# Two causal attention passes: a diagonal of four key tiles walked in three steps instead of four, in a loop unrolled over six groups

## The chip, the cores and the metric

One core of one Trainium2 chip runs the whole program. The metric is device microseconds (us) of one execution, lower is better.

## What is computed

Four residual stages on x of shape (8, 1024, 256): latent attention with softmax, a squared-ReLU MLP, an attention with a quadratic feature map, a ternary linear layer. The two attentions share one function of the kernel:

```python
scores = jnp.einsum('bqhd,bkhd->bhqk', Q, K) / math.sqrt(D_K)     # 16 heads of 16, 1024 positions
scores = jnp.where(causal, scores, -jnp.inf)
attn = jax.nn.softmax(scores, axis=-1)                            # first attention
out = jnp.einsum('bhqk,bkhd->bqhd', attn, V)
# second attention: features are the products x_i x_j, so phi_q . phi_k is a squared score,
# summed causally: num = sum_k (q.k)^2 v_k, den = sum_k (q.k)^2
```

## The kernel before

`attend_pass` works in 32 units (n), one for every batch and group of four heads. A unit holds 1024 queries in two halves h of 512 columns and eight key tiles kt of 128. Transposed scores (128 keys by up to 512 queries, one PSUM bank a head) are made for one **step**, which is one pair (h, kt). There are twelve: for h = 0 the tiles 0 to 3, all on the diagonal, 512, 384, 256 and 128 live columns wide (`q0(s)` is the first live one); for h = 1 the tiles 0 to 3 full, then 4 to 7 of 512, 384, 256 and 128. Engines hand over by semaphores, each engine's order is written out by hand:

- TensorE (PE), in iteration s of `unit`: `scores(s + 2, 0)` for heads 0 and 1, `scores(s + 2, 1)` for heads 2 and 3 (L996, bf16), then `weigh(s)`, the product of the weights with V (L1010, float32, four heads side by side in column groups). AHEAD = 2 steps lie between.
- ScalarE (ACT): `weights(s)` (L893), Exp in the first attention and Square in the second, two instructions a step; `take_sums` (L885) copies the output bank of a half to `osb` when the half's last `weigh` is done. In the order of ACT it stands behind `weights(n + 1, 1)`.
- GpSimd (POOL): one `affine_select` (L866) for each step that holds a diagonal block, eight a unit, on 128 columns of four heads; `weigh` waits for it.
- VectorE (DVE), second attention: the fourth head's square, as a copy (L925) and a product (L928). Steps use three pairs of score banks in turn.
- DVE, first attention: row maxima for the softmax of a later unit. PE makes 36 chunks of 512 columns a unit (`maximum_scores`, L985) into a ring of SRING = 3 banks, DVE reduces them (L946, L948), then `largest` (L954 to L962) finishes a unit's maxima.
- The chunks of later units are dealt into the PE program, one after each `scores` and each `weigh`, three a step. In unit n the first 18 belong to unit n + 1, the last 18 (EARLY = 9 pairs) to unit n + 2. Chunk 18 waits for the load of unit n + 2.
- SyncE (SP), in unit n: wait for the last `weigh` of unit n - 1, 15 transfers of unit n + 2 (L808; q and k parts, then `vs`), store of half 0 (L819), in the first attention 8 small transfers `load_rows` (L815) that carry the maxima to the operands of unit n + 1 once `largest` is done, store of half 1. PE waits for these rows before `scores(n + 1, 0)`.

`all_units` (L790) is a hardware loop of 10 trips with three units written out in each, since the operand tiles rotate by three, and two more units behind it.

Of the kernel before, what the change touches and what calls it, by code (L numbers as in the profile page):

```python
# [703 lines left out]
def attend_pass(nc, z, m, first, softmax):  # L704
# [7 lines left out]
    ROUNDS = (UNITS - 2) // RING  # L712
    assert UNITS == RING * ROUNDS + 2
    ROWS = STACK + 2 if softmax else STACK
# [6 lines left out]
    SLOTS = 4  # L721

# [8 lines left out]
    assert CH == 3 * STEPS  # L731
    SRING = 3
    EARLY = 9
    with ExitStack() as ctx:
# [45 lines left out]
        def q0(s):  # L780

            h, kt = steps[s]
            return max(0, kt * P - h * 512)

        def score_bank(s, hd):
            return 2 * ((2 * s + hd // 2) % PAIRS) + hd % 2

        def all_units(eng, unit):

            with eng.Fori(0, ROUNDS) as i:  # L790
                for r in range(RING):
                    unit(RING * i + r, r, i, True, True)
            unit(UNITS - 2, 0, ROUNDS, True, False)
            unit(UNITS - 1, 1, ROUNDS, False, False)

        @block.sync
        def _(sp):
# [23 lines left out]
            def unit(n, r, rnd, ahead, far):  # L821
# [23 lines left out]
        def _(pool):  # L845
# [14 lines left out]
            def unit(n, r, rnd, ahead, far):  # L860
                for d, s in enumerate(DIAG):
                    if not softmax:
                        pool.wait_ge(d_ready, STEPS * n + s + 1 + DR)
                    wait_alone(pool, p_ready, 2 * STEPS * n + 2 * s + 2 + PR, m.alone)
                    diag = p[s % SLOTS][:, :, q0(s):q0(s) + P]
                    pool.affine_select(out=diag, in_=diag, compare_op=ALU.is_ge, fill=0.0, base=0,  # L866
                                       pattern=[[0, HPU], [1, P]], channel_multiplier=-1).then_inc(masked, 1)
# [4 lines left out]
        def _(act):  # L872
# [9 lines left out]
            def take_sums(n, h):  # L882
                act.wait_ge(pv_done, STEPS * n + (4, STEPS)[h] + PV)
# [3 lines left out]
            def weights(n, s):  # L887
                act.wait_ge(pv_done, STEPS * n + s + 1)
                for k in range(2):
                    act.wait_ge(st_ready, 2 * STEPS * n + 2 * s + k + 1)  # L890
                    heads = 2 if softmax or k == 0 else 1
                    at = score_bank(s, 2 * k)
                    act.activation(p[s % SLOTS][:, 2 * k:2 * k + heads, q0(s):512], m.psum[:, at:at + heads, q0(s):512],  # L893
                                   ACT.Exp if softmax else ACT.Square, scale=z.DK ** -0.5).then_inc(p_ready, 1)

            def unit(n, r, rnd, ahead, far):
                for s in range(STEPS):
                    if s + AHEAD < STEPS:
                        weights(n, s + AHEAD)
                    elif ahead:  # L900
                        weights(n + 1, s + AHEAD - STEPS)
                    if s == 3:
# [3 lines left out]
            for s in range(AHEAD):  # L906
                weights(0, s)
# [3 lines left out]
        def _(dve):  # L911
# [5 lines left out]
            if not softmax:  # L917
                dve.sem_inc(d_ready, DR)

                def unit(n, r, rnd, ahead, far):  # L920

                    for s in range(STEPS):
                        dve.wait_ge(st_ready, 2 * STEPS * n + 2 * s + 2)
                        bank = m.bank[score_bank(s, 3)][:, q0(s):512]
                        dve.tensor_copy(twin[s % 2][:, q0(s):512], bank).then_inc(twin_ready, 1)  # L925
                        dve.wait_ge(pv_done, STEPS * n + s + 1)
                        dve.wait_ge(twin_ready, STEPS * n + s + 1)
                        dve.scalar_tensor_tensor(out=p[s % SLOTS][:, 3, q0(s):512], in0=bank, scalar=1.0 / z.DK,  # L928
                                                 in1=twin[s % 2][:, q0(s):512], op0=ALU.mult, op1=ALU.mult
# [35 lines left out]
            def unit(n, r, rnd, ahead, far):  # L965
# [12 lines left out]
        def _(pe):  # L978
# [10 lines left out]
            def scores(n, r, s, k):  # L989
                h, kt = steps[s]  # L990
# [3 lines left out]
                for hd in (2 * k, 2 * k + 1):  # L994
                    live = operand_rows(hd)
                    last = pe.matmul(m.bank[score_bank(s, hd)][:, q0(s):512], ks[r][live, hd, kt * P:(kt + 1) * P],  # L996
                                     qs[r][live, hd, h * 512 + q0(s):(h + 1) * 512], start=True, stop=True)
                last.then_inc(st_ready, 1)

            def weigh(n, r, s):  # L1000
# [833 lines left out]
```

## Time and profile before

| | us |
|---|---|
| median of 3 runs (2956.73 to 2960.54) | 2957.39 |
| the profiled execution's own time | 2961.86 |
| its span, first to last instruction | 2959.7 |
| mean granted clock of TensorE | 0.938 |
| first attention (a_ tiles), loop and tail | about 300 to 1216 |
| second attention (b_ tiles), loop and tail | about 2087 to 2692 |

The engines are PE (matmul), PEld (weight load, overlaps PE), DVE, ACT, POOL and SP. Matmuls are pipelined and their ends are modelled, so the starts of two neighbouring groups, not their lengths, say what a group takes. In the timeline, "idle before" with a releaser is the engine's own idle time and what ended it; "issue" means that nothing the profile shows was waited for.

### The profile page before, as it was taken

The numbers are of one execution on the slowest core, as the hardware profiler recorded it, in microseconds if no ns is written. First come the engines' busy times: TensorE is split into PE (matmuls) and PEld (weight loads), VectorE is DVE, ScalarE is ACT, GpSimd is POOL, SyncE is SP. The second block draws the span as 40 slices with busy tenths as digits, with TensorE's granted clock in tenths as the row PEclk, the third lists the DMA queues.
The fourth block names the chain that finished last, engine by engine and source line by source line (L and its number), as shares of the span: only waits on it lengthen the run. The fifth ranks groups of instructions, "written<-read, shape, count | busy, mean of one in ns | idle before, by whom it ended". The sixth has DMA issues, their size and how long they took to land. (4 is left out here: it accounts for less than half of the span.)

```text
span 2959.7 us, 60061 instructions
## 1 busy us (share of the span) xinstructions
PE 2508.8 (85%) x15239; PEld 1160.4 (39%) x15239; DVE 2276.6 (77%) x5893; ACT 1784.9 (60%) x2938; POOL 577.6 (20%) x650
## 2 busy tenths in 40 slices
PE   2687999999999999577999978884899999995656
PEld 1342333333333333254666655553222222222545
DVE  5887888888888888286777767997667666665968
ACT  0452666666666666315777747664677777773446
POOL 0445111111121111230000001222222222222300
PEclk9897999999999999888999999997899999997879
DMA  5495232332323322240000003445644444442403
GB/s 169 155 286 187 83 92 89 91 93 86 107 80 100 94 86 79 85 168 1 0 0 0 0 1 100 156 146 167 161 142 141 137 136 139 140 127 99 142 15 113
DMA packets 243316, 309.97 MB, mean 105 GB/s; under 512 B 39472, under 2 KB 177408, under 8 KB 243200
## 3 DMA queue, kind: packets, MB, share of 16 engines
q1 hardware_dynamic: 242752, 307.50, 33.6%
q10 hardware_dynamic: 448, 1.31, 0.2%
q14 instruction: 91, 0.75, 0.1%
q8 instruction: 25, 0.41, 0.1%
HBM read 181.29 MB, written 126.88 MB: 104 GB/s over the span
## 5 line engine op out<-in xcount | busy, mean ns | idle before, releaser
L893 ACT ACTIVATE a_p<-psum 128x1024 f32<-128x1024 f32 (+3 forms) x768 | 588.1, 813 | 303.0 <-PE psum L996 298.4
L893 ACT ACTIVATE b_p<-psum 128x512 f32<-128x512 f32 (+5 forms) x768 | 453.5, 654 | 164.4 <-PE psum L996 163.5
L948 DVE CUSTOM_DVE_ANT_0 a_dump<-psum,a_bias 128x128 bf16<-128x128 f32 (+3 forms) x1024 | 445.6, 487 | 105.7 <-PE psum L985 74.4
L996 PE MATMUL psum<-b_qs,b_ks 96*128 96x512 bf16 (+7 forms) x1536 | 320.9, 330 | 36.0 <-DMA b_vs<-values 35.7
L946 DVE TENSOR_REDUCE a_peak<-psum 128x1 f32<-128x512 f32 x512 | 326.1, 685 | 21.7 <-PE psum L985 20.2
L1010 PE MATMUL psum<-b_p,b_vs 128*32 128x512 f32 (+3 forms) x3072 | 328.5, 499 | 8.0 <-POOL b_p L866 8.0
L925 DVE COPY b_twin<-psum 128x512 f32<-128x512 f32 (+3 forms) x384 | 213.5, 556 | 146.6 <-PE psum L996 144.9
L985 PE MATMUL psum<-a_ks,a_qs 112*128 112x128 bf16 (+2 forms) x1008 | 294.0, 336 | 37.9 <-DVE a_peak L948 19.9
L866 POOL TENSOR_SCALAR_AFFINE_SELECT a_p<-a_p 128x512 f32<-128x512 f32 x256 | 162.4, 635 | 767.2 <-ACT a_p L893 767.2
L866 POOL TENSOR_SCALAR_AFFINE_SELECT b_p<-b_p 128x512 f32<-128x512 f32 x256 | 162.4, 634 | 455.2 <-DVE b_p L928 440.2
L996 PE MATMUL psum<-a_qs,a_ks 114*128 114x512 bf16 x1008 | 248.0, 328 | 3.4 <-ACT a_p L893 1.8
L928 DVE SCALAR_TENSOR_TENSOR b_p<-psum,b_twin 128x512 f32<-128x512 f32 (+3 forms) x384 | 214.5, 558 | 40.0
L996 PEld LDWEIGHTS psum<-b_qs,b_ks 96*128 96x128 bf16 (+1 forms) x1536 | 110.1, 98 | 339.9 <-issue 173.7
L1444 PE MATMUL psum<-f_xt,w_fc 128*128 128x512 f32 x512 | 223.9, 595 | 4.7 <-ACT f_hid L1385 2.8
L1010 PE MATMUL psum<-a_p,a_vs 128*32 128x512 f32 x2016 | 218.8, 507 | 0.6 <-POOL a_p L866 0.4
L1246 PE MATMUL psum<-wo,m_att 128*128 128x256 f32 x512 | 142.3, 441 | 77.0 <-POOL m_att L1193 74.1
L1580 POOL TENSOR_TENSOR g_parts<-g_rest,g_parts 128x2048 bf16<-128x2048 f32 x16 | 65.2, 4074 | 667.1 <-DVE g_parts L1568 667.1
L985 PEld LDWEIGHTS psum<-a_ks,a_qs 112*128 112x128 bf16 x1008 | 87.2, 97 | 260.3 <-DVE a_peak L948 124.4
L985 PE MATMUL psum<-first_k,first_q 112*128 112x128 bf16 (+3 forms) x528 | 159.3, 348 | 30.1 <-DMA first_v<-values 16.6
L1455 PE MATMUL psum<-w_proj,f_parts 128*128 128x256 bf16 x1536 | 170.3, 273 | 1.4 <-DVE f_scaled L1333 1.4
L1455 PEld LDWEIGHTS psum<-w_proj,f_parts 128*128 128x128 bf16 x1536 | 150.2, 98 | 19.4 <-DVE f_scaled L1333 1.7
L1246 PEld LDWEIGHTS psum<-wo,m_att 128*128 128x128 f32 x512 | 112.8, 226 | 102.8 <-issue 52.4
(202 smaller groups left out, 3752.8 us busy)
## 6 DMA issues: line engine op xcount, KB each, us to landing
qk_parts<-l_parts SPq DMA_DIRECT2D x96, 256.0 KB
qk_parts<-g_parts SPq DMA_DIRECT2D x96, 256.0 KB, 2.8
b_qs<-qk_parts SPq DMA_DIRECT2D x160, 128.0 KB, 2.9
b_ks<-qk_parts SPq DMA_DIRECT2D x155, 128.0 KB, 2.9
values<-l_vx SPq DMA_DIRECT2D x64, 256.0 KB
sums<-a_osb SPq DMA_DIRECT2D x64, 256.0 KB, 2.4
m_num<-sums SPq DMA_DIRECT2D x64, 256.0 KB
m_inv<-reciprocals SPq DMA_DIRECT2D x64, 256.0 KB
```

Source lines behind the costliest of these rows:

```text
L866: pool.affine_select(out=diag, in_=diag, compare_op=ALU.is_ge, fill=0.0, base=0, pattern=[[0, HPU], [1, P]], channel_multiplier=-1).then_i ...
L893: act.activation(p[s % SLOTS][:, 2 * k:2 * k + heads, q0(s):512], m.psum[:, at:at + heads, q0(s):512], ACT.Exp if softmax else ACT.Square, ...
L925: dve.tensor_copy(twin[s % 2][:, q0(s):512], bank).then_inc(twin_ready, 1)
L928: dve.scalar_tensor_tensor(out=p[s % SLOTS][:, 3, q0(s):512], in0=bank, scalar=1.0 / z.DK, in1=twin[s % 2][:, q0(s):512], op0=ALU.mult, op ...
L946: last = dve.tensor_reduce(dst, piece, AX.X, ALU.max)
L948: last = dve.tensor_tensor_reduce(dump[c % SRING][:, at:at + w], piece, bias[:, 512 - w:], 1.0, NEG, ALU.add, ALU.max, dst)
L985: last = pe.matmul(m.bank[SB + c % SRING][:, at:at + w], qs[r][0:TOP, hd, qt * P:(qt + 1) * P], ks[r][0:TOP, hd, h * 512:h * 512 + w], sta ...
L996: last = pe.matmul(m.bank[score_bank(s, hd)][:, q0(s):512], ks[r][live, hd, kt * P:(kt + 1) * P], qs[r][live, hd, h * 512 + q0(s):(h + 1) ...
L1010: last = pe.matmul(m.bank[OB[h]][32 * hd:32 * hd + 32, q0(s):512], vs[r][:, kt, 32 * hd:32 * hd + 32], p[s % SLOTS][:, hd, q0(s):512], sta ...
L1246: last = pe.matmul(bank, att[u][:, c, t * P:(t + 1) * P], wo[:, c, :], start=(c == 0), stop=(c == DC - 1))
L1444: last = pe.matmul(m.bank[F0 + j % 4], m.w_fc[:, c, j * P:(j + 1) * P], xt[u][:, c, :], start=(c == 0), stop=(c == DC - 1))
L1455: last = pe.matmul(bank, parts[u][:, part, j, t * P:(t + 1) * P], m.w_proj[:, j, :], start=(part == j == 0), stop=(part == PARTS - 1 and j ...
```

## The change

Steps 1 and 3 of a diagonal (384 and 128 columns) become one step of 512: its bank holds tile kt + 1 in columns 128 to 512 and tile kt + 3 in columns 0 to 128. The order of a diagonal is full, merged, 256. Ten steps a unit instead of twelve. One ACT pair, one DVE pair and one `pv_done` serve both pieces; PE still issues a matmul for each piece and head, POOL still masks each diagonal block on its own, so a merged step has two masks, the second behind a wait for the first. Chunks of the maxima are dealt (1, 2, 1) to eight steps and (1, 1, 0) to the two narrow ones; the first 20 of a unit belong to unit n + 1, the last 16 (EARLY = 8) to unit n + 2. Four weight tiles and three bank pairs no longer repeat within one unit or three, so the loop has 5 trips of six units.

```diff
-    ROUNDS = (UNITS - 2) // RING
-    steps = [(h, kt) for h in range(2) for kt in range(4 * (h + 1))]
+    LONG = 2 * RING
+    ROUNDS = (UNITS - 2) // LONG
+    def full(h, kt):
+        return h, ((kt, 0, 0, 512),)
+    def edge(h):
+        kt = 4 * h
+        return [full(h, kt), (h, ((kt + 1, 128, 128, 384), (kt + 3, 0, 384, 128))), (h, ((kt + 2, 256, 256, 256),))]
+    steps = edge(0) + [full(1, kt) for kt in range(4)] + edge(1)
     STEPS = len(steps)
-    DIAG = [s for s, (h, kt) in enumerate(steps) if kt >= 4 * h]
+    LAST = (2, STEPS - 1)
+    DIAG = [[at for kt, at, q, w in pieces if kt >= 4 * h] for h, pieces in steps]
+    MASKS = [sum(len(d) for d in DIAG[:s + 1]) for s in range(STEPS)]
...
-    EARLY = 9
+    EARLY = 8
+    MOST = [(1, 1, 0) if s in LAST else (1, 2, 1) for s in range(STEPS)]
...
             with eng.Fori(0, ROUNDS) as i:
-                for r in range(RING):
-                    unit(RING * i + r, r, i, True, True)
+                for v in range(LONG):
+                    unit(LONG * i + v, v, 2 * i + v // RING, True, True)
...
-                for d, s in enumerate(DIAG):
+                for s in range(STEPS):
+                    if not DIAG[s]:
+                        continue
                     if not softmax:
                         pool.wait_ge(d_ready, STEPS * n + s + 1 + DR)
                     wait_alone(pool, p_ready, 2 * STEPS * n + 2 * s + 2 + PR, m.alone)
+                    for k, at in enumerate(DIAG[s]):
+                        if k:
+                            wait_alone(pool, masked, MASKS[-1] * n + MASKS[s] - 1, m.alone)
+                        diag = slot(v, s)[:, :, at:at + P]
+                        pool.affine_select(out=diag, in_=diag, compare_op=ALU.is_ge, fill=0.0, base=0,
+                                           pattern=[[0, HPU], [1, P]], channel_multiplier=-1).then_inc(masked, 1)
...
                 for hd in (2 * k, 2 * k + 1):
                     live = operand_rows(hd)
+                    for kt, at, q, w in pieces:
+                        last = pe.matmul(m.bank[score_bank(v, s, hd)][:, at:at + w], ks[r][live, hd, kt * P:(kt + 1) * P],
+                                         qs[r][live, hd, h * 512 + q:h * 512 + q + w], start=True, stop=True)
...
-                if s in DIAG:
-                    pe.wait_ge(masked, len(DIAG) * n + DIAG.index(s) + 1)
+                if DIAG[s]:
+                    pe.wait_ge(masked, MASKS[-1] * n + MASKS[s])
...
+                for kt, at, q, w in pieces:
+                    for hd in range(HPU):
+                        last = pe.matmul(m.bank[OB[h]][32 * hd:32 * hd + 32, q:q + w], vs[r][:, kt, 32 * hd:32 * hd + 32],
+                                         slot(v, s)[:, hd, at:at + w], start=(kt == 0), stop=(s == LAST[h]),
+                                         skip_group_check=True)
...
+                    late = CH - 2 * EARLY
+                        if k < late and ahead:
+                            maximum_scores(n + 1, (r + 1) % RING, 2 * EARLY + k, 2 * EARLY + k + 1)
+                        if k >= late and far:
+                            if k == late:
+                                pe.wait_ge(loaded[(r + 2) % RING], LOADED * (rnd + (r + 2) // RING) + LOADED)
+                            maximum_scores(n + 2, (r + 2) % RING, k - late, k - late + 1)
...
+                    for k in range(3):
+                        if k == 2:
+                            weigh(n, v, s)
+                        elif there:
+                            scores(*at, k)
+                        some_maxima(dealt, MOST[s][k])
+                        dealt += MOST[s][k]
```

## Rows read from the trace of the kernel before

**Rows 1.** By stretch: length, PE, PEld, DVE, ACT, POOL busy (x), PEclk, DMA, GB/s
```profile
346.00:1185.50 839.50, 787.35 (x5574) 282.55 (x5578) 715.23 (x2437) 554.77 (x755) 147.22 (x232) 0.98 0.30 90
573.20:576.60 3.40, 3.40 (x15) 1.02 (x8) 2.33 (x13) 0.74 (x1) 0.52 (x1) 0.50 0.66 188
655.70:740.20 84.50, 79.78 (x577) 28.95 (x576) 73.64 (x253) 57.20 (x79) 15.07 (x25) 1.00 0.31 94
2297.97:2354.55 56.58, 55.86 (x432) 15.94 (x433) 39.35 (x73) 44.69 (x79) 15.22 (x24) 1.00 0.46 139
```

**Rows 2.** L954 from 340 to 1190 us: once a unit
```profile
L954 DVE TENSOR_REDUCE a_npeak<-a_peak x30: 220/220/221, 346.0 to 1185.5; 128x32 f32<-128x64 f32 x30
```

**Rows 3.** Waits from 400 to 1170 us: us in total, times, longest
```profile
DVE a_dump L948 <- issue: 21.9, 14, 2.8
PE psum L985 <- DMA first_v<-values: 14.9, 9, 2.0
```

**Rows 4.** Timeline of the first attention, from one unit's load to its use
```profile
623.59 0.64 PE L1010 MATMUL psum<-a_p,a_vs 128*32 128x256 f32 x8
626.31 0.60 ACT L885 ACTIVATE a_osb<-psum 128x512 f32<-128x512 f32 x1
627.80 0.63 SPq L808 DMA_DIRECT2D a_qs<-qk_parts  x1
637.47 0.44 SPq L808 DMA_DIRECT2D a_vs<-values  x1
641.68 4.99 SPq L815 DMA_DIRECT2D first_q<-a_rows  x8
642.19 0.39 PE L985 MATMUL psum<-a_ks,a_qs 112*128 112x128 bf16 x2 [2.04 <-DMA a_vs<-values]
650.54 0.39 PE L985 MATMUL psum<-a_ks,a_qs 112*128 112x512 bf16 x1
652.16 0.64 PE L1010 MATMUL psum<-a_p,a_vs 128*32 128x256 f32 x8
```

**Rows 5.** DMA issues from 400 to 1170 us: KB each, median us to landing
```profile
q14 instruction: 51, 0.42, 0.2%
a_qs<-a_rows SPq DMA_DIRECT2D x144, 2.0 KB, 1.8
```

**Rows 6.** Timeline behind two ends of a trip, first attention
```profile
572.00 0.39 PE L985 MATMUL psum<-a_ks,a_qs 112*128 112x512 bf16 x1 [1.98 <-DVE a_peak L948]
...
658.27 0.29 DVE L948 CUSTOM_DVE_ANT_0 a_dump<-psum,a_bias 128x128 bf16<-128x128 f32 x1 [2.50 <-issue]
```

**Rows 7.** Timeline of the second attention, one full step, then the end of a unit
```profile
2305.88 1.06 PE L1010 MATMUL psum<-b_p,b_vs 128*32 128x512 f32 x8
2306.88 1.04 PE L996 MATMUL psum<-b_qs,b_ks 96*128 96x512 bf16 x4
2307.85 1.06 PE L1010 MATMUL psum<-b_p,b_vs 128*32 128x512 f32 x8
2307.95 0.69 DVE L925 COPY b_twin<-psum 128x512 f32<-128x512 f32 x1 [0.48 <-PE psum L996]
2308.75 0.69 DVE L928 SCALAR_TENSOR_TENSOR b_p<-psum,b_twin 128x512 f32<-128x512 f32 x1
2309.68 0.63 POOL L866 TENSOR_SCALAR_AFFINE_SELECT b_p<-b_p 128x512 f32<-128x512 f32 x1 [8.72 <-DVE b_p L928]
2315.55 0.43 PE L1010 MATMUL psum<-b_p,b_vs 128*32 128x128 f32 x8
2316.83 1.07 PE L1010 MATMUL psum<-b_p,b_vs 128*32 128x512 f32 x8 [0.24 <-POOL b_p L866]
```

**Rows 8.** DMA queues from 2140 to 2650 us: the only line of part 3
```profile
q1 hardware_dynamic: 28192, 71.14, 45.8%
```

**Rows 9.** ACT from 400 to 1170 us by shape: busy, mean ns
```profile
L893 ACT ACTIVATE a_p<-psum 128x1024 f32<-128x1024 f32 x323 | 315.9, 1026 | 142.5 <-PE psum L996 142.3
L893 ACT ACTIVATE a_p<-psum 128x768 f32<-128x768 f32 x107 | 81.0, 808 | 29.1 <-PE psum L996 25.2
```

More of the change, by code:

```diff
@@ L819, in store, with unit @@
                 sp.dma_start(m.sums_dram[bass.ts(n, P), h * 512:(h + 1) * 512], osb[h][:, :]).then_inc(stored[h], 16)
-            def unit(n, r, rnd, ahead, far):
+            def unit(n, v, rnd, ahead, far):
+                r = v % RING
                 if far:
@@ L858, in _, with unit @@
                 pool.wait_ge(k_set, 2)
-            def unit(n, r, rnd, ahead, far):
-                for d, s in enumerate(DIAG):
+            def unit(n, v, rnd, ahead, far):
+                for s in range(STEPS):
+                    if not DIAG[s]:
+                        continue
                     if not softmax:
@@ L906, in _ @@
             for s in range(AHEAD):
-                weights(0, s)
+                weights(0, 0, s)
             all_units(act, unit)
@@ L963, in largest, with unit @@
                               ).then_inc(rows_ready, 1)
-            def unit(n, r, rnd, ahead, far):
+            def unit(n, v, rnd, ahead, far):
+                r = v % RING
                 if ahead:
@@ L987, in maximum_scores, with scores @@
                     last.then_inc(s_ready, 1)
-            def scores(n, r, s, k):
-                h, kt = steps[s]
+            def scores(n, v, s, k):
+                h, pieces = steps[s]
+                r = v % RING
                 pe.wait_ge(p_ready, 2 * STEPS * n + 2 * s + k + 1)
@@ L995, in scores, with weigh @@
                     live = operand_rows(hd)
[L996 to L997 removed]
+                    for kt, at, q, w in pieces:
+                        last = pe.matmul(m.bank[score_bank(v, s, hd)][:, at:at + w], ks[r][live, hd, kt * P:(kt + 1) * P],
+                                         qs[r][live, hd, h * 512 + q:h * 512 + q + w], start=True, stop=True)
                 last.then_inc(st_ready, 1)
[L1000 to L1001 removed]
+            def weigh(n, v, s):
+                h, pieces = steps[s]
+                r = v % RING
                 pe.wait_ge(p_ready, 2 * STEPS * n + 2 * s + 2 + PR)
@@ L1018, in operands, with unit, some_maxima @@
                     pe.wait_ge(rows_loaded[r], ROWS_LOADED * rnd + ROWS_LOADED)
-            def unit(n, r, rnd, ahead, far):
-                def some_maxima(k):
+            def unit(n, v, rnd, ahead, far):
+                r = v % RING
+                def some_maxima(first, count):
                     if not softmax:
                         return
-                    half = CH // 2
-                    if k < half and ahead:
-                        maximum_scores(n + 1, (r + 1) % RING, half + k, half + k + 1)
-                    if k >= half and far:
-                        if k == half:
-                            pe.wait_ge(loaded[(r + 2) % RING], LOADED * (rnd + (r + 2) // RING) + LOADED)
-                        maximum_scores(n + 2, (r + 2) % RING, k - half, k - half + 1)
+                    late = CH - 2 * EARLY
+                    for k in range(first, first + count):
+                        if k < late and ahead:
[4 more added lines that the diff above has]
+                            maximum_scores(n + 2, (r + 2) % RING, k - late, k - late + 1)
+                dealt = 0
                 for s in range(STEPS):
```

69 lines of the change are left out of this document (28 added, 41 removed).

## The prediction

> **What bounds the kernel now.** First I read the busy time of one trip in each attention [rows 1]. In the second attention PE works 55.86 of 56.58 us for three units, 18.86 a unit; ACT has 44.69 and DVE 39.35. Only PE sets the pace there. In the first, PE works 79.78 of 84.50 us and DVE 73.64: neither is full, and the waits must say what the rest is.
>
> A unit of the first attention is the distance between two L954: 29 in 839.5 us, 28.95 each [rows 2]. It has three kinds of loss. PE stands up to 2.0 us before a chunk until the `vs` transfer has landed [rows 3]; the row shown has 9 cases with 14.9 us, that of the other buffers as many, so this comes in two units of three. DVE stands up to 2.8 us for "issue", 21.9 us over the eight trip ends of that stretch [rows 3]; the timeline shows it is the jump back of the loop, 2.50 us that nothing in the program ended, and PE then waits for DVE, 1.98 us in another trip [rows 6]. The two don't add up: where a trip end has held PE, the load has landed meanwhile. Third, behind some of these stalls the granted clock falls: after the 1.98 us at 572.00 it is 0.50 (1.2 GHz, else 2.4) from 573.2 to 576.6 [rows 1, 6]. Over the 29 units it is 0.98 [rows 1]: 4% of the time at half rate, 34 us, which cost half of that, 17 us.
>
> The load's chain is in [rows 4]. Let T be the end of a unit's last `weigh` but one: it starts at 623.59, its 256 columns take 0.46, T = 624.05. ACT reaches `take_sums` at 626.31 (T + 2.26), SP starts the 15 transfers at 627.80, issues the last at 637.47, and PE goes on at 642.19, T + 18.1, after 2.04 us of idle. With the mean stall of 14.9 / 9 = 1.65 it is T + 17.7. From there to the next T (652.16 + 0.46 = 652.6) are 10.4 us without a stall: 28.1 for a unit inside a trip. A unit behind a trip end has the 2.4 us of the jump instead of the 1.65: about 28.9. Check: 19 x 28.1 + 10 x 28.9 + 17 = 840, as measured.
>
> **First attention.** I count PE work in blocks of 512 columns, 0.213 us at 2.4 GHz. A step costs 0.26 us above its columns: 8 blocks in 2307.85 - 2305.88 = 1.97 us [rows 7]. About 0.07 of it belong to the matmuls; 0.19 are the two changes between scores and float32 product, which a merged step pays once for both pieces.
>
> *Removed:* two steps' changes, 0.38 us of PE a unit. The columns stay (108 blocks with the maxima).
>
> *Where the first chunk of unit n + 2 stands.* Before, PE reached it 18.1 - 2.04 = 16.1 us after T. After, 68 blocks stand between T and chunk 20: 8 of iteration 9, then 10, 12, 8, 12, 12 and 6 of iteration 5; 14.5 us, with six steps' extra 16.1. PE arrives at the same time. The load arrives later: ahead of `take_sums` ACT now has `weights(n + 1, 1)` at 1024 elements instead of 768, 1026 against 808 ns twice [rows 9], and its scores end later: 0.5 us. T to chunk 20 becomes 18.2, the stall about 2.
>
> *From there to the next T* are left 6 blocks of iteration 5, then 12, 10 and 11: 39 blocks, 8.3 us, 1.0 extra, 9.3 instead of 10.4. A unit inside a trip takes 27.5 instead of 28.1: PE stands still for the load with more of the unit done.
>
> *Trip ends.* Ten become five; I take 29.6 us for such a unit. The jump costs DVE the same 2.5. SP's chain, if its doubled loop has to be fetched too, adds up to 2.5 to the load. And the rows begin to bind: SP starts them at 641.68, the last is issued at 646.1 and lands 1.8 us later [rows 4, 5], near 647.6, 5.4 us after PE went on; PE asks at 650.54 now, 8.35 us after it went on, and 6.7 after the change. With a load stall ahead 1.3 us remain; without one about 1 us is missing.
>
> Over 29 units: 24 x 27.5 + 5 x 29.6 = 808 against 823, -15. Two chunks fewer ahead of the loop and four exponentials fewer in the last unit: -2. The clock: stalls of 2 us in 25 units instead of 1.65 in 20 let it fall somewhat more often; its price was 17 us for ten trip ends and twenty load stalls, I add +3 (bounds 0 and +15). **First attention: -14.**
>
> **Second attention.** *PE:* 72 blocks are 15.36 us, twelve steps' extra make 18.48; the 0.38 up to 18.86 are the wait of `weigh(0)` for its mask, at 2316.83 and in each unit [rows 7]. After: 18.10, and that wait goes, since 12 blocks instead of 8 stand between the scores of step 0 and `weigh(0)`.
>
> *A new wait, the merged step's two masks.* From the end of its scores (2306.88 + 0.87) it is 0.20 to the copy, 0.80 to the product, 0.93 to POOL, 0.63 for a mask [rows 7], a gap in which POOL waits for itself, 0.63, and 0.14 to PE. The gap isn't in these rows: below it is 0, above the 0.24 from DVE's end to POOL's start (2308.75 + 0.69 to 2309.68); I take 0.24, since it is a semaphore wait as well: 3.6 us. Between the scores of the unit's first merged step and its `weigh` PE has 12 blocks, with the changes 3.15 us: a stall of 0.4 (0.2 with no gap). The second has 14 blocks: none. Unit: 18.5 instead of 18.86; 31 units, **-11**. ACT (15 us a unit) and DVE (13) stay below.
>
> *The loop's body.* Of this I am least sure. A trip now issues 577 + 576 matmuls and weight loads in the first attention and 432 + 433 in the second [rows 1], plus some 60 waits a unit by the code. DVE issues 253 in the first and with its waits, two for each of 108 chunks and more, near 480. PE, ACT and SP stand nowhere at their jumps; DVE in the first attention does at each. The stretch of the first holds 51 instruction fetches [rows 5], that of the second none [rows 8]. So a short body stays inside an engine and a long one is fetched at each trip. Doubled, PE's is 2,300 + 340 and 1,730 + 300, more than any that stays here; ACT, SP and the second attention's DVE come to 300 to 360, between the 200 that stay and the 480 that doesn't. For PE's jump the bounds are 0, if it stays, and DVE's 2.8 at most in these rows; I take 2.5, by the nearest row. In the first attention it lies beside DVE's. In the second nothing hides it: 5 x 2.5 = +12.5, and the clock, which fell behind about a third of the long stalls, adds 1.7 in some: +3. The other engines' fetches fall into the same 2.5 us. **Together +4.5.**
>
> The Trainium skill, "Runtime: NRT & Kernel Launch", section "Instruction fetch mechanics", says that TensorE keeps 2048 instructions and the others 512, filled in order, and that a jump to a target outside stalls the engine. By that the first attention's body on PE falls out and the second's, about 2,030, could just stay; this sum would end 15.5 us lower. The trace agrees that a short body isn't fetched again, but DVE's of about 480, under the page's 512, is.
>
> **Sum.** -14 + 4.5 = -9.5 us; other stages are untouched. The terms come from an execution with a span of 2959.7 and a time of 2961.9, 4.5 above the median of 2957.4. Set against the median: 2948.
>
> **Rivals.**
> 1. *PE's doubled body stays in the second attention.* For it: no body of PE has fallen out so far. Against: it would be the longest of all by far. -9.5 - 15.5: 2932. Chance 0.18, with the page above for it.
> 2. *Jumps cost more.* Behind the first fetched block comes a second stall, or the stalls of PE, DVE, SP and ACT follow one another: 5 us instead of 2.5 in ten trip ends, +13 to +25: 2961 to 2973, slower. It decides from about 4 us a jump. For it: a longer body has more fetches. Against: DVE's never exceeds 2.8 [rows 3]. Chance 0.15.
> 3. *The rows become the bound.* Between the last chunk of a unit's maxima and its first scores PE has 6.9 us; the chain is 1.0 for that chunk, 1.1 for `largest`, 5.9 to the last landing, 8.0. It decides when the load stall ahead of it falls under 1 us or DVE is late by as much: +1 us in 25 units, 2973. For it: four chunks a step are 2.6 us of DVE in 2.8 of PE. Against: the load stall falls just there. Chance 0.08.
> 4. *The masks stall both merged steps*, with a gap of 0.6: +0.7 a unit, 2970. Chance 0.06.
>
> The forecast has 0.53, its own range is 2940 to 2956. Eight in ten: from rival 1, 2930, to where rivals 2 to 4 begin, 2965. 0.2% is 5.9 us, about what a measurement of this kernel can tell from none. Faster (below 2951.5): rival 1 and two thirds of the forecast, and a tenth of the others, 0.57. Slower (above 2963.3): most of rivals 2 to 4 at their high ends, 0.18. The same: 0.25.
>
> **What the profile after would show.** In the second attention: full steps 1.97 us apart as before, no wait of `weigh(0)` for POOL, one of 0.4 us before `weigh(1)`, units of 18.5; at five trip ends a PE gap of about 2.5 us, with instruction fetches in the loop. In the first: units of 27.5 inside a trip with a `vs` wait of about 2 us, five DVE gaps of 2.5, L815 landing before PE asks. The prediction is wrong if a wait for rows stands before the scores of each unit, if PE has no gap at its jumps, or if the gaps are 5 us.

## The result

The changed kernel takes 2995.6 us (median of 4 runs, 2978.6 to 3000.1) against 2957.1 (4 runs): ratio 1.012 [1.0085, 1.0155]. It is slower by 38.5 us between the medians, where 2948 was forecast, and it lies outside the range, above the price of every rival too (2973 at most). The profiled execution is the fastest of the four: 2978.6 us, span 2976.9, only 17.2 more than the span before. The other runs lie 16 to 22 us above it; most of this spread gets an explanation below.

The copies of the output bank (`a_osb` and `b_osb`) frame each attention. Before, first and last start of the 64:

```profile
L885 ACT ACTIVATE a_osb<-psum x64: 597/603/628, 313.6 to 1216.0; 128x512 f32<-128x512 f32 x64
L885 ACT ACTIVATE b_osb<-psum x64: 597/603/605, 2096.1 to 2692.1; 128x512 f32<-128x512 f32 x64
```

After:

```profile
L905 ACT ACTIVATE a_osb<-psum x64: 597/605/606, 310.6 to 1238.7; 128x512 f32<-128x512 f32 x64
L905 ACT ACTIVATE b_osb<-psum x64: 597/605/608, 2116.1 to 2711.6; 128x512 f32<-128x512 f32 x64
```

The first attention took 902.4 us and takes 928.1; the second took 596.0 and takes 595.5. So +25.7 and -0.5, where -14 and +4.5 were forecast. What lies around them is 8 us shorter in this execution: 1453.3 us for 1461.3. A second profile of the same kernel (e4_again below) has 1463.0 there, so this is no effect of the change.

Windows with the same columns as in [rows 1], after (a stretch of the first attention; the 3.4 us behind a PE gap in the second and in the first; one unit of the second; one trip of six units of the first):

```profile
346.00:1185.50 839.50, 767.80 (x5422) 284.16 (x5426) 717.97 (x2380) 521.30 (x621) 144.40 (x228) 0.97 0.30 90
2222.20:2225.60 3.40, 3.40 (x15) 0.76 (x14) 1.09 (x3) 0.87 (x2) 1.91 (x3) 0.51 0.16 55
856.60:860.00 3.40, 3.40 (x18) 1.31 (x11) 1.81 (x9) 0.88 (x1) 0.00 (x0) 0.54 0.04 3
2183.30:2201.60 18.30, 18.14 (x149) 5.75 (x146) 12.74 (x21) 14.67 (x24) 4.99 (x8) 1.00 0.45 145
657.00:837.90 180.90, 165.17 (x1152) 60.83 (x1152) 152.70 (x504) 111.05 (x132) 31.01 (x49) 0.96 0.29 89
```

A trip of the first attention has 1152 + 1152 = 2,304 matmuls and weight loads on PE. One of the second, six units, has 1,728:

```profile
2220.30:2334.00 113.70, 109.98 (x864) 34.36 (x864) 76.78 (x122) 88.31 (x134) 30.03 (x49) 0.98 0.46 141
```

The granted clock fell to half in the second attention too, where before it stood at 1.00.

Waits from 400 to 1170 us, to be held against [rows 3]:

```profile
PE psum L1008 <- DMA a_vs<-values: 30.6, 17, 3.7
PE psum L1008 <- DMA first_v<-values: 16.1, 9, 2.2
```

And the second attention, 2140 to 2650 us. "issue" at the first scores of a trip is PE's jump; at one of the four jumps the profile names DVE instead, which came last:

```profile
PE psum L1021 <- issue: 7.5, 3, 3.0
PE psum L1037 <- POOL b_p L886: 3.9, 23, 0.2
PE psum L1021 <- DVE b_p L950: 3.1, 1, 3.1
```

In the first attention PE now waits for the load in 26 of 27 units instead of two of three. The wait for a jump is there in both attentions, once a trip (in the first 9.9 us, 4 times, at most 3.3). DVE's own jump no longer shows: before, DVE stood 21.9 us for "issue" in that stretch [rows 3], now 0.8, since it waits for PE instead. The instruction queues of the second attention's stretch, against none in [rows 8]:

```profile
q8 instruction: 41, 0.67, 0.6%
q14 instruction: 64, 0.52, 0.3%
```

Over the whole program q8 carries 121 packets of 16 KB instead of 25, and in the first kernel with three units a trip (below) it falls back to 25. I take it to be PE's: before, where DVE alone stood at its jumps, 51 fetches came by q14 [rows 5] and none by q8. No trace names the engine.

An end of a trip in the second attention, then one in the first and the load behind it:

```profile
2202.00 0.61 ACT L905 ACTIVATE b_osb<-psum 128x512 f32<-128x512 f32 x1
2216.32 1.22 POOL L886 TENSOR_SCALAR_AFFINE_SELECT b_p<-b_p 128x512 f32<-128x512 f32 x2 [0.16 <-POOL b_p L886]
2220.24 0.60 ACT L905 ACTIVATE b_osb<-psum 128x512 f32<-128x512 f32 x1
2222.02 0.87 PE L1021 MATMUL psum<-b_qs,b_ks 96*128 96x256 bf16 x4 [2.21 <-issue]
2242.09 0.60 ACT L905 ACTIVATE b_osb<-psum 128x512 f32<-128x512 f32 x1
...
836.32 0.60 ACT L905 ACTIVATE a_osb<-psum 128x512 f32<-128x512 f32 x1
837.91 0.39 PE L1021 MATMUL psum<-first_q,first_k 114*128 114x256 bf16 x2 [2.01 <-issue]
840.73 0.66 SPq L822 DMA_DIRECT2D a_qs<-qk_parts  x1
842.71 0.62 SPq L822 DMA_DIRECT2D a_ks<-qk_parts  x1
855.98 0.39 PE L1008 MATMUL psum<-a_ks,a_qs 112*128 112x128 bf16 x2 [3.67 <-DMA a_vs<-values]
870.03 0.60 ACT L905 ACTIVATE a_osb<-psum 128x512 f32<-128x512 f32 x1
```

A unit of the second attention takes 2220.24 - 2202.00 = 18.24 us; across the trip end it is 21.85. In the first, the unit across the trip end takes 33.7: 28.1, 2.0 for the jump, some 2 more of the load stall (3.67 instead of the 1.54 below) and 1.7 for the clock, which falls behind that stall. The load is late because SP, behind its own jump, starts it 4.4 us after the output copy (836.32 to 840.73) instead of 1.5, and its second transfer comes 2.0 us behind the first instead of 0.8; that SP's program was being fetched meanwhile fits, but no row shows it.

The load chain, in a unit inside a trip (against [rows 4]):

```profile
924.84 1.07 PE L1037 MATMUL psum<-a_p,a_vs 128*32 128x384 f32 x16
928.53 0.60 ACT L905 ACTIVATE a_osb<-psum 128x512 f32<-128x512 f32 x1
930.02 0.65 SPq L822 DMA_DIRECT2D a_qs<-qk_parts  x1
940.01 0.44 SPq L822 DMA_DIRECT2D a_vs<-values  x1
944.21 0.39 PE L1008 MATMUL psum<-a_ks,a_qs 112*128 112x128 bf16 x2 [1.54 <-DMA a_vs<-values]
947.38 1.06 PE L1037 MATMUL psum<-a_p,first_v 128*32 128x512 f32 x8
950.12 1.06 PE L1037 MATMUL psum<-a_p,first_v 128*32 128x512 f32 x8
952.98 1.07 PE L1037 MATMUL psum<-a_p,first_v 128*32 128x384 f32 x16
```

The merged `weigh` has four blocks, so T is 924.84 and some 0.9, 925.7. PE goes on at T + 18.5, and the next T is 9.7 behind it: 28.1 again, not 27.5. This is a short unit of the changed kernel. Of the 30 distances between the second copies of neighbouring units, the four across a trip end add up to 132.6 us, and the other 26 to 756.7, 29.1 each.

### The profile page after: what moved, and what is told of

It reads as the page before. It is cut to its first block and busy times, and to the rows that moved or that the text cites. A ratio compares the mean times of both kernels' runs of the same rounds, so it can differ in the third digit from the quotient of the medians.

```text
span 2976.9 us, 58458 instructions
## 1 busy us (share of the span) xinstructions
PE 2495.8 (84%) x15239; PEld 1182.2 (40%) x15239; DVE 2280.2 (77%) x5765; ACT 1755.5 (59%) x2682; POOL 575.4 (19%) x650
## 5 line engine op out<-in xcount | busy, mean ns | idle before, releaser
L914 ACT ACTIVATE a_p<-psum 128x1024 f32<-128x1024 f32 (+1 forms) x640 | 568.0, 942 | 346.8 <-PE psum L1021 346.6
L914 ACT ACTIVATE b_p<-psum 128x512 f32<-128x512 f32 (+2 forms) x640 | 444.2, 749 | 171.0 <-PE psum L1021 167.8
L1021 PE MATMUL psum<-b_qs,b_ks 96*128 96x512 bf16 (+7 forms) x1536 | 311.5, 332 | 47.2 <-DMA b_vs<-values 36.5
L968 DVE TENSOR_REDUCE a_peak<-psum 128x1 f32<-128x512 f32 x512 | 333.4, 687 | 22.6 <-PE psum L1008 19.8
L947 DVE COPY b_twin<-psum 128x512 f32<-128x512 f32 (+1 forms) x320 | 204.0, 637 | 162.8 <-PE psum L1021 159.2
L1037 PE MATMUL psum<-b_p,b_vs 128*32 128x512 f32 (+3 forms) x3072 | 318.5, 502 | 5.9 <-POOL b_p L886 5.8
L1008 PE MATMUL psum<-a_ks,a_qs 112*128 112x128 bf16 (+2 forms) x1008 | 279.3, 338 | 40.4 <-DMA a_vs<-values 35.5
L1021 PE MATMUL psum<-a_qs,a_ks 114*128 114x512 bf16 x1008 | 237.7, 332 | 7.9 <-issue 3.6
L950 DVE SCALAR_TENSOR_TENSOR b_p<-psum,b_twin 128x512 f32<-128x512 f32 (+1 forms) x320 | 204.3, 638 | 36.4 <-PE psum L1037 2.3
L1037 PE MATMUL psum<-a_p,a_vs 128*32 128x512 f32 x2016 | 207.1, 498 | 0.5 <-POOL a_p L886 0.3
```

Source lines behind the costliest of these rows:

```text
L914: act.activation(slot(v, s)[:, 2 * k:2 * k + heads, cols], m.psum[:, at:at + heads, cols], ACT.Exp if softmax else ACT.Square, scale=z.DK ...
L947: dve.tensor_copy(twin[s % 2][:, cols], bank).then_inc(twin_ready, 1)
L950: dve.scalar_tensor_tensor(out=slot(v, s)[:, 3, cols], in0=bank, scalar=1.0 / z.DK, in1=twin[s % 2][:, cols], op0=ALU.mult, op1=ALU.mult). ...
L968: last = dve.tensor_reduce(dst, piece, AX.X, ALU.max)
L1008: last = pe.matmul(m.bank[SB + c % SRING][:, at:at + w], qs[r][0:TOP, hd, qt * P:(qt + 1) * P], ks[r][0:TOP, hd, h * 512:h * 512 + w], sta ...
L1021: last = pe.matmul(m.bank[score_bank(v, s, hd)][:, at:at + w], ks[r][live, hd, kt * P:(kt + 1) * P], qs[r][live, hd, h * 512 + q:h * 512 + ...
```

## Experiments: the loop's body

Theory: the doubled body costs the time. Rival: the merged steps do. Three kernels, and the changed one once more:

```diff
# e1_short: changed kernel, three units a trip, a fifth weight tile
-    LONG = 2 * RING
-    SLOTS = 4
+    LONG = RING
+    SLOTS = 5
# e2_oldlong: changed kernel with the twelve old steps, EARLY = 9 and three chunks a step; six units a trip
# e3_second: first attention as before (old steps, three units a trip), second as in e1_short
# e4_again: the changed kernel
```

> The changed kernel with a fifth weight tile in both attentions, so that its ten steps repeat after three units and the loop has ten trips of three units again. Theory A (the doubled loop body is what makes it slower: every engine fetches its body again at each of four jumps): the second attention has units of 18.24 us throughout and no instruction fetches, 19 us less than the changed kernel; the first attention loses its four units of about 33 us and gets nine of about 29.5, some 5 us less. Together about 2960 to 2970, or 3 to 10 us above the kernel before. Theory B (the merged steps themselves are slower in the first attention, the loop costs little): the first attention stays 20 us or more above the kernel before, the second falls below it by 19, total about 2955 to 2960. Theory C (everything comes from the body): at or below 2940.

> The twelve steps of the kernel before, dealt as before, in the loop of six units: the body alone. Theory A: the second attention has units of 18.86 us with four jumps of 3.6 to 5.7 us each, +19; the first attention has four trip ends of 4 us instead of nine of 2.4, about 0; total 2975. Theory B (the merged steps are the cost): near 2957 in the first attention, the second +19 all the same. The part of the first attention tells: above 905 us between its first and last output copy would put its loss on the body, 895 to 905 on the steps.

> The first attention as in the kernel before (twelve steps, three units a trip); only the second has the ten steps, with five weight tiles and three units a trip. Theory A and B alike: units of 18.24 instead of 18.86 in the second attention and no fetches there, 31 x 0.62 = 19 us less than before: 2938. If the fifth tile or the two masks cost more at short trips than at long ones, less is gained.

> The changed kernel once more, for a second profile. Its unprofiled runs were 16 to 21 us above the profiled one. Theory D (the clock falls behind load stalls of about 2 us, and how often it does differs from run to run): this profile shows another number of half-clock stretches in the first attention than the 13 of the first, and its time moves by about 1.7 us for each. If the number is the same and the time differs, something else varies (waits for the rows, the jumps).

| | median, range (runs) | ratio to before | first att. | second att. |
|---|---|---|---|---|
| e1_short | 2944.8, 2939.4 to 2951.6 (10) | 0.9947 [0.9926, 0.9969] | 906.3 | 576.9 |
| e2_oldlong | 3024.8, 3020.4 to 3025.5 (4) | 1.0207 [1.0159, 1.0255] | 942.1 | 616.3 |
| e3_second | 2937.2, 2929.9 to 2947.7 (7) | 0.9912 [0.9885, 0.9939] | 908.3 | 576.9 |
| e4_again | 3007.7, 2997.6 to 3017.9 (2) | 1.0154 [1.0082, 1.0227] | 956.9 | 596.4 |

The two last columns are the distance of first and last output copy in the profiled run, as for e1_short here:

```profile
L905 ACT ACTIVATE a_osb<-psum x64: 597/603/603, 312.3 to 1218.6; 128x512 f32<-128x512 f32 x64
L905 ACT ACTIVATE b_osb<-psum x64: 598/604/607, 2097.4 to 2674.3; 128x512 f32<-128x512 f32 x64
```

Two of the four went otherwise than expected: e1 came out at 2944.8, below the totals of its theories A and B, and e2 lost 40 us in the first attention, where about none was expected, and ended 50 us above its forecast. The profiled run is the slowest of its kernel in e2, e3 and e4, near the median in e1.

In the second attention it comes apart cleanly: merged steps alone -19.1 us (576.9 for 596.0), the loop of six alone +20.3 (e2), both together -0.5. In the first, merged steps alone are worth nothing: +3.9, while the old first attention took 902.4 before and 908.3 in e3, and between the medians e1 is 7.6 us slower than e3, which has the old steps there. The loop of six alone costs 40, both 26 and, in the second execution, 54. The second execution shows where the spread of the changed kernel comes from. Window and waits of e4_again:

```profile
346.00:1185.50 839.50, 756.78 (x5239) 278.38 (x5231) 695.34 (x2298) 505.32 (x601) 138.87 (x219) 0.95 0.30 88
```

```profile
PE psum L1008 <- DMA a_vs<-values: 44.0, 17, 5.3
PE psum L1008 <- DMA first_v<-values: 16.9, 8, 2.7
```

The clock record of the traces has it to the stretch. In the first attention the clock stood at half in 9 stretches before, 30.7 us together; in 14 in the changed kernel, 47.8 us; in 24 in e4, 88.7 us. At half rate half of the time is lost where PE is what everything waits for, so at most 15, 24 and 44 us. Of the 28.7 us between the two executions up to 20 are therefore the clock, as theory D had it (another number of falls), and PE's load wait is 14 us longer as well (60.9 for 46.7).

The same record makes e1 and the changed kernel comparable. From 400 to 1170 us all of PE's waits together are 49.6 us in e1 and 61.0 in the changed kernel, only 11 more: e1's are 67 short ones, for DVE, rows and load, the changed kernel's mostly 26 long ones for the load. The clock stood at half in 2 stretches of e1, 6.8 us, which is up to 20 us less than in the changed kernel. Of the 22 us between them (928.1 for 906.3) the waits can thus be 11 at most, and half or more is the clock.

## Experiments: the wait for the load, and no jump at all

Theory: in the first attention the doubled body hurts through the load stall. Before, a DVE jump in every third unit held PE and the load landed meanwhile; with trip ends only in every sixth, the stall stands in nearly every unit, and the clock falls behind it. (The traces show a second reason, told below: SP issues the load more slowly.) The first chunk of unit n + 2 needs only q and k, yet waits for the v tile, the last and largest transfer:

```diff
# e5_vs: changed kernel; e6_vs_short: e1_short; e8_vs_second: e3_second
-        LOADED = 16 * 15
+        LOADED = 16 * 14
-                for dst, src in pairs:
+                for dst, src in pairs[:-1]:
                     sp.dma_start(dst, src).then_inc(loaded[r], 16)
+                sp.dma_start(*pairs[-1]).then_inc(v_loaded[r], 16)
             def operands(n, r, rnd):
                 pe.wait_ge(loaded[r], LOADED * rnd + LOADED)
+                pe.wait_ge(v_loaded[r], 16 * rnd + 16)
# e7_line: changed kernel (load as it was), thirty units in one trip
-    LONG = 2 * RING
+    LONG = 10 * RING
```

> The changed kernel, with the 15th transfer of a load (the v tile) on a semaphore of its own, which PE waits for only before the next unit's scores; the first chunk of unit n + 2 waits for the 14 q and k transfers. Theory A (in the first attention the doubled body costs mostly through the load stall: with DVE no longer late at the trip ends, PE waits about 2 us for the load in nearly every unit, and the granted clock falls behind many of these waits): the wait of about 2 us in 29 units and most of the 14 to 24 clock falls go; what is left are four trip ends with their falls: first attention 895 to 910 us between its first and last output copy (928 and 957 before this edit), whole kernel 2950 to 2975. Theory B (the extra time is the trip ends and something in all units that belongs to the merged steps): the stall turns into a wait for the rows or for DVE, first attention still 920 to 955, kernel 2980 to 3005. The second attention is the same in both, 596.

> The ten merged steps with the loop of three units and five weight tiles (2944.8 us), with the v transfer on its own semaphore as above. If the load wait is what matters in the first attention (20 us of stall in 15 units): 892 to 900 us instead of 906, kernel 2932 to 2940. If DVE and the rows are the bound there (25 and 10.5 us of waits): the stall moves to them, first attention 902 to 908, kernel 2940 to 2947.

> The changed kernel with all thirty units written out, one trip, so no jump back is taken inside an attention. Theory A (a body that does not stay costs at the jump alone, since straight code is fetched ahead of its use): second attention 577 us as in the loop of three units with merged steps, first attention about 905 to 930 (load stall and clock falls stay, the four trip ends of 33 to 35 us go), kernel 2930 to 2960. Theory B (continuous fetching itself slows PE or the loads): second attention 585 or more with units above 18.24, kernel 2975 or more.

> First attention with the twelve old steps and the loop of three units, second with the ten merged steps, five weight tiles and the loop of three units (2937.2 us), with the v transfer on its own semaphore. The wait for the load (35 us in 21 units) and the clock falls behind it (12, 41 us at half rate) are what it should remove. If the load is the bound: first attention 885 to 895 us instead of 908, kernel 2915 to 2927. If DVE is: 900 to 908, kernel 2930 to 2937.

| | median, range (runs) | ratio to before | first att. | second att. |
|---|---|---|---|---|
| e5_vs | 2968.9, 2958.8 to 2979.5 (10) | 1.0018 [0.9999, 1.0036] | 909.2 | 593.9 |
| e6_vs_short | 2944.9, 2941.9 to 2947.2 (6) | 0.9931 [0.9909, 0.9954] | 905.0 | 576.9 |
| e7_line | 2931.7, 2927.3 to 2933.2 (4) | 0.9885 [0.9855, 0.9914] | 888.9 | 578.0 |
| e8_vs_second | 2910.7, 2909.6 to 2919.2 (5) | 0.9820 [0.9795, 0.9846] | 870.5 | 576.9 |

These kernels ran beside a kernel before of 2963.8 us, those above beside one of 2961.0 and those below beside one of 2957.8, so medians of different tables compare only to a few us; the ratios allow for it.

e5 against e6 is the six-unit loop without the wait for v: +4.2 us in the first attention, where with it (changed kernel against e1) it was +22 and +51. So the load wait with the clock falls behind it carried most of the first attention's loss; the jumps, set against five fewer DVE jumps, carry about 4. The clock stood at half in 4 stretches instead of 14 and 24. The wait for the load is not gone in e5, it is 18.4 us instead of 46.7 and 60.9, now for the last k transfer (400 to 1170 us):

```profile
PE psum L1011 <- DMA a_ks<-qk_parts: 12.7, 12, 2.3
PE psum L1011 <- DMA first_k<-qk_parts: 5.7, 5, 2.0
```

In the second attention e5 still pays 17.0.

In the second attention e7 shows that only the jump costs, not the fetching. Its instruction queues from 2140 to 2600 us are busy, yet its only PE wait there is the one for masks, and units are 18.3. In its first attention PE stands 0.4 us for "issue" once a unit (10.6 us, 24 times), at the scores that need the rows; whether that is the rows or a fetch is not told apart there. For the rows speaks that e11 and e12 (below), which fetch as much and get their rows earlier, have no such wait.

```profile
q8 instruction: 30, 0.49, 0.5%
q14 instruction: 19, 0.16, 0.1%
```

```profile
PE psum L1037 <- POOL b_p L886: 5.0, 25, 0.2
```

The Trainium skill, "Runtime: NRT & Kernel Launch", section "Instruction fetch mechanics", says the same: straight code is streamed, a taken branch to a target that is no longer held stalls. The trace agrees on both; a body on PE of 1,728 counted instructions, and up to 354 waits by the kernel's text (59 a unit), was fetched at each jump. So its length is between 1,728 and 2,082, on both sides of the page's 2048 instructions, by which the prediction let the body just stay, and no run here tests that figure.

For the first attention e7 is no clean test of the jump. There the load wait was expected to stay without jumps, and the attention to take 905 to 930 us; it took 888.9, and the load wait shrank to 9.7 us. SP's rows show a reason. A load of the changed kernel, 928.53 to 940.01 above, is issued to its v transfer in 11.5 us from the output copy; one of e7 in 9.5:

```profile
812.71 0.60 ACT L905 ACTIVATE a_osb<-psum 128x512 f32<-128x512 f32 x1
813.79 0.59 SPq L822 DMA_DIRECT2D a_qs<-qk_parts  x1
822.19 0.58 SPq L822 DMA_DIRECT2D a_vs<-values  x1
```

Over the loads from 400 to 1130 us, the median from copy to first transfer is 1.5 us in every loop and 1.1 in straight code (e7, e11, e12). From first transfer to v it is 9.6 to 9.7 in all loops of three (never above 9.9), 10.0 and 10.4 in the two profiles of the changed kernel, 10.3 and 10.2 in e2 and e5 (up to 12.0), and 8.4 to 8.7 in straight code. So the long body delays the load inside its trips too, by some 0.3 to 0.8 us, and straight code brings it some 1.5 us earlier; why SP is faster there isn't shown. How much of the load stall comes from this and how much from the missing DVE jumps of the theory was not separated.

e6 came out by its second branch (905.0 us, the stall moves to DVE and rows), and e8, better than either of its branches, shows why. The same edit is worth 38 us with old steps (908.3 to 870.5 in the profiled runs, both the slowest of their kernels; 26 between the medians) and 1 us with merged ones. The waits of e6_vs_short, 400 to 1170 us:

```profile
PE psum L1011 <- DVE a_peak L973: 33.0, 66, 1.4
PE psum L1024 <- DMA a_qs<-a_rows: 12.3, 18, 1.3
PE psum L1024 <- DMA first_q<-a_rows: 1.6, 8, 0.2
```

Where the load no longer holds PE, the rows do, in 26 units of 27, and DVE. In its timeline:

```profile
666.96 0.22 DVE L979 TENSOR_REDUCE a_npeak<-a_peak 128x32 f32<-128x64 f32 x1
668.37 4.99 SPq L831 DMA_DIRECT2D a_qs<-a_rows  x8
674.64 0.60 PE L1024 MATMUL psum<-a_qs,a_ks 114*128 114x512 bf16 x2 [0.29 <-DMA a_qs<-a_rows]
```

7.7 us from `largest` to the scores. The shortest units take 28.0 to 28.2 us with the load wait (changed kernel, e1) and without it (e5, e6): behind the load stood a chain of the same length.

## Experiments: the deal

Two things in the new deal could be at fault: iterations 0 and 7 get four chunks beside narrow scores, 10 blocks or 2.38 us of PE against 2.6 of DVE (they take 2.74, as from 947.38 to 950.12 above); and the last chunk of the next unit's maxima stands only 6.9 us of PE work ahead of the scores that need the rows.

```diff
# e9_deal: e6_vs_short; e10_deal9: e9 and EARLY = 9
-    MOST = [(1, 1, 0) if s in LAST else (1, 2, 1) for s in range(STEPS)]
+    MOST = [(1, 1, 1) if s in (0, 2, 7, 9) else (1, 2, 1) for s in range(STEPS)]
-    EARLY = 8
+    EARLY = 9
# e11_line_old: e8_vs_second with LONG = 10 * RING, SLOTS = 4
# e12_line_deal: e10_deal9 with LONG = 10 * RING, SLOTS = 4
```

> Merged steps, loop of three units, v transfer on its own semaphore (2944.9 us; first attention 905.0, 28.1 us the undisturbed unit, of which PE works 26.7), with the chunks dealt otherwise: three instead of four to the two iterations that make narrow scores beside full weights (0 and 7), three instead of two to the two that weigh the narrow step (2 and 9). Theory A: four chunks are 2.6 us of DVE and those two iterations have 10 blocks, 2.38 us of PE, and took 2.74; the even deal gives 0.7 us a unit back: undisturbed unit about 27.3, first attention 885 to 895 us, kernel 2925 to 2935. Theory B: the rows (asked for 8 us behind the last chunk, 6.9 us of PE work between) set the pace, and a shorter way there only makes that wait longer: unit stays at 28.1, kernel 2940 to 2947.

> The even deal and EARLY = 9: the maxima of unit n + 1 are complete two chunks earlier, at the end of iteration 4, and PE has one more iteration (about 2.7 us) of work before it asks for the rows. If theory B above is right this is where the gain comes: unit 26.9 to 27.2, first attention 868 to 880 us, kernel 2907 to 2920. If the rows were not the bound: as the even deal alone. The first chunk of unit n + 2 comes two chunks earlier and may wait for the q and k transfers: if so about 0.5 to 1 us a unit is lost again.

> First attention with the twelve old steps, second with the ten merged ones, v transfer on its own semaphore (2910.7 us in a loop of three units, first attention 870.5, units of 26.5 and trip ends of 30.4), with thirty units written out in one trip. If the jump is all that a trip end costs: ten times 3.9 us go, first attention 832 to 842 us, kernel 2873 to 2885. If straight code that is fetched on the way costs something of its own, or the rows and loads bind once DVE no longer falls behind: 842 to 860, kernel 2885 to 2902.

> Merged steps in both attentions, even deal, EARLY = 9, v transfer on its own semaphore, thirty units written out. Beside the run before it (old steps in the first attention) this is merging in the first attention by itself, with no jump and no wait for the v tile. By the prediction's sum a merged unit has 0.38 us of PE less than an old one: 820 to 832 us. If two more small matmuls a head and four chunks a step eat that up (PE busy 26.7 against 26.5 a unit in the last runs): the same as the old steps or up to 15 us more, 835 to 855.

| | median, range (runs) | ratio to before | first att. | second att. |
|---|---|---|---|---|
| e9_deal | 2954.6, 2947.4 to 2969.7 (10) | 0.9992 [0.9971, 1.0014] | 914.5 | 576.6 |
| e10_deal9 | 2903.4, 2898.0 to 2911.7 (4) | 0.9812 [0.9787, 0.9838] | 862.2 | 576.9 |
| e11_line_old | 2879.7, 2875.6 to 2888.5 (5) | 0.9743 [0.9719, 0.9768] | 835.5 | 577.9 |
| e12_line_deal | 2885.6, 2885.3 to 2889.0 (4) | 0.9762 [0.9738, 0.9786] | 847.0 | 578.0 |

The even deal alone gained nothing, it lost 9 us against e6 (0.6% by the ratios), more than either theory had. In e9 the wait for rows doubles, the sign of theory B:

```profile
PE psum L1024 <- DMA a_qs<-a_rows: 22.1, 18, 1.8
PE psum L1024 <- DMA first_q<-a_rows: 5.9, 8, 0.8
```

With the maxima complete two chunks earlier (e10) the rows' wait is all but gone, 2.4 us in one unit, the wait for DVE falls from 36.2 to 21.4 us, the shortest units take 26.6 us instead of 28.0, and the first attention is 52 us shorter, 6 us better than the best expected. So with the load wait out of the way, the rows were the bound of the merged first attention, with EARLY = 8. Whether EARLY = 9 alone, without the even deal, would do was not run.

e11 and e12 differ only in the first attention's steps, deal and places of the chunks. Windows 400 to 1100 us, e11 then e12:

```profile
400.00:1100.00 700.00, 697.73 (x5045) 249.63 (x5044) 644.21 (x2212) 495.46 (x683) 134.30 (x212) 1.00 0.34 99
```

```profile
400.00:1100.00 700.00, 683.28 (x4991) 261.99 (x4984) 647.98 (x2182) 479.30 (x572) 131.95 (x208) 1.00 0.34 99
```

With old steps PE is full. With merged ones it is not: the saving in PE turns into waits for DVE (9.0 us, 46 times) and rows. Merging in the first attention costs 11.5 us there (5.9 between the medians); in a loop of three units with the even deal and EARLY = 9 it is 8 us shorter than with old steps (e10 against e8), where the trip ends weigh as well, but by the ratios, 0.9812 and 0.9820, these two are not told apart. e11 is the best version: merged steps in the second attention alone, v tile on its own semaphore, units written out. It beats before by 2.6%. e11 and e12 came out within what was expected.

## Why the prediction was wrong, step by step

- *Direction*: faster was forecast, by 9.5; it is slower, by 17 in the profiled executions and by 38.5 between the medians. The second attention's net (+4.5, measured -0.5) came near by luck, two errors that cancel in part (-8.1 in the steps, +3.1 in the jumps); the first attention's (-14, measured +25.7 and +54.5) is what failed: a unit inside a trip, the trip end and the clock were all priced too low.
- *Second attention, steps*: right, and too small: -11 was forecast, -19.1 measured in e1. The unit is 18.24 instead of 18.5: `weigh(0)`'s wait went, and the two masks cost 0.17 us a unit (3.9 us in 23), not 0.4, since POOL's gap between them is 0.16 and not 0.24. Without it PE needs 18.07 where 18.10 was summed, but that is luck: the wait that went was 0.24 us (6.1 us in 25 units before, 2140 to 2600), not the 0.38 read from the sum, and a merged step saved 0.27 us, all of a step's extra, instead of 0.19. **Rival 4 fell.**
- *Second attention, jumps*: the mechanism was right, the size was not. +15.5 was forecast for five; a loop of five trips jumps back four times, and these cost 18.6 (e1 to the changed kernel), 4.65 each instead of 3.1. PE's gap is 2.2 to 3.1; the rest is the clock behind it, which fell at all four instead of some and stood at half for 20.5 us, and perhaps engines that are late after it. **Rival 1 fell. Rival 2's price, over 4 us a jump, is met here.** Which of the engines' fetches beside PE's counts was not separated.
- *First attention, a unit inside a trip (27.5)*: 28.1 at best. T to the end of the load wait was well put (18.2 forecast, 18.5 in the unit shown; that SP is slower inside a long trip was not in it). From there 9.3 was forecast and 9.7 measured: the iteration with 10 blocks was summed as PE work, 2.38, and took 2.74, while DVE was busy with its chunks almost without a gap. 0.6 us in 24 units is some 15 us, all that was forecast as gain. Nor would 27.5 have come without the load stall: the shortest units of e5 and e6 take 28.0 to 28.1 too. With clock falls and longer load waits the 26 units took 29.1 on average, where the forecast with its 20 us of clock has 28.2.
- *First attention, trip ends (29.6)*: 33.7 in the unit shown. It was right that SP would be late with the load there; the step failed in adding nothing for the sequence: PE's jump, then the late load, then the clock. The five DVE gaps of 2.5 us that the jump was to lie beside are not in the profile; PE's own gaps, 2.0 to 3.3, stand in their place. The four such units take 32.6, 33.6, 33.7 and 32.7 us between copies, 14 us above the forecast for four.
- *The clock in the first attention (+3)*: up to +8.5 in the profiled run (47.8 us at half instead of 30.7) and up to +29 in the next (88.7); the bound was +15. In the profiled run the unit and the trip ends weigh more; in the next, and by their times in the other runs, this is the step by which the size of the loss was missed: it was seen that the stall would stand in 25 units instead of 20, and its price was taken for nearly fixed.
- *Rival 3, the rows*: not the bound in the changed kernel (4.0 us of waits for rows from 400 to 1170, beside 46.7 for the load), but true behind it, at the point that was given: e6 took the load stall away and the rows held PE. 8.0 us were forecast for the chain against 6.9 of PE work. (Its last landing is 0.3 us too early: 646.1 and 1.8 are 647.9, not 647.6.)

What the runs show: the doubled loop is the loss (e1 against the changed kernel, e2 against before), in the second attention through the jump, in the first mostly through the load wait (e5), and there at least as much through the clock that falls behind it as through the stall (changed kernel to e5: 9 us less of PE's waits, 61.0 to 52.1, and up to 17 less of clock, for 18.9 in all). What decides behind which stall the clock falls stays open.

## What to carry to other kernels

Before a loop body is lengthened, count each engine's instructions in it, and multiply the taken jumps (trips less one) by the stall, the late engines and the clock behind it. Where the whole can be written out, straight code cost 1.1 us in the second attention, and without its nine trip ends the first was 35 us shorter (e8 to e11; 31 between the medians, 23 by the ratios), where trip ends had taken some 3.9 us each above a unit of 26.5. When a change evens out or removes one stall, list the waits that it was covering (here the load, behind it the rows) with their slack, since a gain in PE work is only paid where PE is full. A consumer that waits for a whole group of transfers should wait for the ones that it reads: splitting off one semaphore was worth 26 to 38 us with old steps, 19 and 48 us of the first attention with merged steps in the loop of six (928.1 and 956.9 to 909.2), and nothing with merged steps in a loop of three, where the rows held PE next.

## What was not expected of the hardware

- In straight code of 288 matmuls and weight loads and up to 59 waits a unit on PE, 30 packets of 16 KB were fetched in 460 us with no wait on PE but the masks'; a jump back in the changed kernel cost 2.0 to 3.3 us of PE gap.
- The cost of a stall varied between executions of one kernel. The changed kernel's first attention took 928 and 957 us, with 14 and 24 falls of the granted clock. The kernels nearly without load waits (e11, e12) had none and one, and e12's four times lay within 4 us, though e11's five within 13.
- SP issued the 15 transfers of a load in 8.4 to 8.7 us in straight code, 9.6 to 9.7 in a loop of three units and 10.0 to 10.4 in a loop of six (medians).
